# Relation attention of a graph kernel: four turns of two heads by 13 or 12 destination blocks in place of five turns of four heads by 5 blocks

## The chip, the cores and the metric

The kernel runs on one core of a Trainium2 chip. The metric is the device time of one execution in microseconds (us). Engines are named as in the profile: PE is TensorE (PEld its weight loads), DVE is VectorE, ACT is ScalarE, POOL is GpSimd, SP is SyncE, which here only issues DMAs.

## The reference

Four graph layers follow each other on 3125 nodes with 128 features and 103125 edges. The change touches the third one alone, an attention with three relations and four heads of 32 features:

```
for r in range(3):
    h = (x @ W[r]).reshape(N, 4, 32)
    a_s, a_d = einsum(h, att_src[r]), einsum(h, att_dst[r])      # [N, 4] each
    score = leaky_relu(a_s[src] + a_d[dst], 0.2); edges of another type masked, self edges kept
    alpha = softmax of score over the edges of a destination, per head
    rel_out = segment_sum(alpha * h[src], dst)
    out = out + softmax(rel_w)[r] * (rel_out + bias[r])
x = layernorm(x + out)
```

## The kernel before

Nodes are cut into 25 blocks of 125. Earlier in the kernel the edges are counted into matrices `K.counts[r]` in DRAM: for each source node (partition), destination block and source block, a row of 128 16-bit counts. Attention is then dense: since leaky_relu has two branches, the exponential of a score is a product of a source factor and a destination factor on either side of a threshold. For each pair of blocks and each head the kernel makes `sel`, the counts where the destination's `ad` is on one side of the source's threshold, and multiplies it on PE with the values `T.mv` (each split in two 16-bit parts); the other side comes as the unmasked counts `ct` times the values less the same.

For each of the three relations (tags `r0`, `r1`, `r2`) `gat` runs `scores` (projection, thresholds, values; it also loads the first `ct` and `ad` tiles), then `attention_heads`, then `relation_sum`, one after the other; each is a block that all engines leave together.

`attention_heads` has five turns, a loop over g. In a turn five destination blocks sit in PSUM banks 0 to 4 (264 columns each, for four heads), and 25 steps run over the source blocks s. In a step

- ACT makes the masks of three heads (two in steps 7, 15 and 23) by a Sigmoid with a very large scale (L936), 640 columns each;
- DVE makes the other one or two heads' `sel` with a compare and multiply of 640 columns (L954) and multiplies the ACT masks with the counts (L958, 1920 or 1280 columns);
- PE runs, for each of the 5 blocks, eight matmuls of 66 columns (four heads, two parts; L1009) and two of 132 columns with the unmasked counts (L1013).

`sel` and `msk` have five slots by step. DVE runs three steps into the next turn and then drains the five banks (L969 multiplies by the destination factors, L976 adds the two halves). PE clears a bank with a matmul of zeros (L1005) at a turn's first step, after that bank was drained. SP loads `ct` in chunks of five source blocks (L925) and the next turn's `ad` (L919).

`relation_sum` divides by the denominators and adds the result to `K.x` (L1061 to L1066); for r0 it also adds the bias (L1070 to L1074).

Of the kernel before, what the change touches and what calls it, by code (L numbers as in the profile page):

```python
# [217 lines left out]
def count_edges(nc, K, S):  # L218
# [12 lines left out]
    with ExitStack() as ctx:  # L231
# [9 lines left out]
        with nc.Block() as block:  # L241
# [48 lines left out]
            def _(pe):  # L290
# [31 lines left out]
                with pe.Else():  # L322
                    pe.sem_inc(wide_used, 1)

                    def five_groups(i):
                        for s in range(OHS):

                            pe.wait_ge(taken, i * OHS + s + 1)
                            pe.matmul(K.ps[:, s, :], K.zeros[:, 0:128], K.zeros[:], start=True, stop=True)
# [7 lines left out]
                            pe.matmul(K.ps[:, s, 0:128], K.zeros[:, 0:128], K.zeros[:, 0:128], start=False, stop=False,  # L337
# [278 lines left out]
def scores(nc, K, S, tag, k, counts, H, F, T):  # L616
# [9 lines left out]
    with ExitStack() as ctx:  # L626
# [17 lines left out]
        with nc.Block() as block:  # L644
# [45 lines left out]
            @block.sync  # L690
            def _(sp):

                for c in range(5):
                    sp.dma_start(T.ct[:, c], counts[:, 0:5, 5 * c:5 * c + 5]).then_inc(T.landed[c], 16)
                sp.wait_ge(adt, 7)
                sp.dma_start(K.ad_rows[0:H], adr[:]).then_inc(adst, 16)
                sp.wait_ge(adst, 16)
                sp.sem_inc(T.ad_landed, 16)
# [55 lines left out]
def attention_one(nc, K, S, tag, counts, F, T, degree=False):  # L754
# [6 lines left out]
    with ExitStack() as ctx:  # L761
# [31 lines left out]
        with nc.Block() as block:  # L793
# [69 lines left out]
            def _(pe):  # L863
                pe.sem_inc(used, 25)
                with pe.Fori(0, 5) as g:
                    for s in range(NB):
# [3 lines left out]
                        for b in range(5):  # L870
                            if s == 0:

                                pe.wait_ge(drained, 5 * g + b + 1)
                                pe.matmul(K.ps[:, b, 0:2 * F], K.zeros[:, 0:128], K.zeros[:, 0:2 * F], start=True,
                                          stop=True)
# [11 lines left out]
def attention_heads(nc, K, S, tag, counts, H, F, T):  # L887
# [7 lines left out]
    AHEAD = 3  # L895
    HF = H * F

    by_act = lambda s: list(range(2 if s % 8 == 7 else 1, H))
    masks = [sum(len(by_act(i)) for i in range(s)) for s in range(NB + 1)]
    with ExitStack() as ctx:  # L900
        sb = lambda name, shape, dt: ctx.enter_context(nc.sbuf_tensor(tag + name, shape, dt))
        ct, ad, landed, ad_landed = T.ct, T.ad, T.landed, T.ad_landed
        sel = sb("sel", [P, 5, H, 5, PAD], F16)
        msk = sb("msk", [P, 5, 3, 5, PAD], F16)
        tmp = sb("tmp", [P, 2, 2 * HF], F32)
        (masked, used, full, scaled, drained, mready, turns) = (
            S(tag + "_" + n) for n in ("masked", "used", "full", "scaled", "drained", "mready", "turns"))
        with nc.Block() as block:
            @block.sync
            def _(sp):  # L910

                with sp.Fori(1, 5) as g:

                    slot, first = sp.snap(g % 2), sp.snap(5 * g)
                    made, had = sp.snap(25 * g + 1), sp.snap(16 * g + 16)
                    ready_first(sp, slot, first, made, had)
                    sp.wait_ge(used, made)
                    sp.wait_ge(ad_landed, had)
                    sp.dma_start(ad[:, bass.ds(slot, 1)].rearrange("p a h d -> p (a h) d"),  # L919
                                 K.ad_rows[0:H, bass.ds(first, 5)].rearrange("h b d -> h (b d)").partition_broadcast(P)  # L920
                                 ).then_inc(ad_landed, 16)
                    for c in range(5):

                        sp.wait_ge(used, 25 * g + 5 * c + 5)
                        sp.dma_start(ct[:, c], counts[:, bass.ds(first, 5), 5 * c:5 * c + 5]).then_inc(landed[c], 16)  # L925

            @block.scalar
            def _(act):
                with act.Fori(0, 5) as g:
                    for s in range(NB):  # L930
                        act.wait_ge(ad_landed, 16 * g + 32)

                        act.wait_ge(masked, 25 * g + s + 1)
                        act.sem_inc(turns, 1)
                        for n, h in enumerate(by_act(s)):
                            act.activation(msk[:, s % 5, n], ad[:, bass.ds(g % 2, 1), h]  # L936
                                           .rearrange("p a (b d) -> p (a b) d", d=PAD),
                                           ACT.Sigmoid, bias=T.thr[:, 1, s, h:h + 1],
# [3 lines left out]
            def _(v):  # L942
                v.sem_inc(drained, 5)
                v.sem_inc(masked, 5)

                def step(g, s):

                    n, c = len(by_act(s)), ct[0:P, s // 5, :, s % 5]
                    v.wait_ge(ad_landed, 16 * g + 32)
                    v.wait_ge(landed[s // 5], 16 * g + 16)  # L950

                    v.wait_ge(used, 25 * g + s + 21)
                    for h in range(H - n):
                        v.scalar_tensor_tensor(  # L954
                            sel[:, s % 5, h], ad[:, bass.ds(g % 2, 1), h].rearrange("p a (b d) -> p (a b) d", d=PAD),
                            T.thr[:, 0, s, h:h + 1], c, ALU.is_lt, ALU.mult)
                    v.wait_ge(mready, masks[NB] * g + masks[s + 1])
                    v.tensor_tensor(sel[:, s % 5, H - n:H], msk[:, s % 5, 0:n],  # L958
                                    c.unsqueeze(1).to_broadcast([P, n, 5, PAD]), ALU.mult).then_inc(masked, 1)

                def drain(g):

                    for b in range(6):
                        if b < 4:
                            v.wait_ge(full, 4 * g + b + 1)
                        elif b == 4:
                            v.wait_ge(used, 25 * g + 50)
                        if b < 5:
                            v.tensor_tensor(tmp[:, b % 2].rearrange("p (x f) -> p x f", f=F),  # L969
                                            K.ps[0:P, b, 0:2 * HF].rearrange("p (x f) -> p x f", f=F),  # L970
                                            T.c[:, bass.ds(5 * g + b, 1)].rearrange("p b h a -> p (b h a)").unsqueeze(2)
                                            .to_broadcast([P, 2 * H, F]), ALU.mult).then_inc(drained, 1)
                        if b > 0:
                            v.wait_ge(drained, 5 * g + b + 5)
                            t4 = tmp[:, (b - 1) % 2].rearrange("p (h a f) -> p h a f", h=H, a=2)
                            v.tensor_tensor(T.num[:, bass.ds(5 * g + b - 1, 1)].rearrange("p b h f -> p (b h) f"),  # L976
                                            t4[:, :, 0], t4[:, :, 1], ALU.add).then_inc(scaled, 1)
                            v.wait_ge(scaled, 5 * g + b)

                for s in range(AHEAD):  # L980
                    step(0, s)
                with v.Fori(0, 4) as g:
                    for s in range(AHEAD, NB):
                        step(g, s)
                    for s in range(AHEAD):
                        step(g + 1, s)
                    drain(g)
                for s in range(AHEAD, NB):
                    step(4, s)
                drain(4)  # L990

            @block.tensor
            def _(pe):
                pe.sem_inc(used, 25)
# [663 lines left out]
```

## Time and profile before

| | |
|---|---|
| median of 3 runs | 2834.3 us (2833.37 to 2838.01) |
| the profiled execution: its time | 2861.55 us |
| its span, first to last instruction | 2859.7 us |
| PE busy | 73% of the span |
| DVE busy | 78% |
| ACT busy | 64% |
| mean granted clock of PE | 0.888 |

The profiled execution is 27 us longer than the median of the runs without a profiler. Sums below are made against its own time. "Busy" counts an instruction from its start to its end; instructions of one engine overlap by a little, so the pitch from start to start is what adds up.

### The profile page before, as it was taken

To read this page: it belongs to the slowest core of one execution; us is meant where nothing else is said; L and a number is where in the kernel's file an instruction comes from. 1 tells how busy PE (TensorE), PEld (TensorE's weight loads), DVE (VectorE), ACT (ScalarE), POOL (GpSimd) and SP (SyncE) were. 2 spreads that over 40 slices of the span, in tenths; PEclk is the share of its full clock that TensorE was granted. 3 is DMA by queue.
4 is the path that set the end of the run, shared out by engine and by line. 5 is a ranking of instruction groups with operands and counts; after the bars stand their busy time and mean duration, and the time that the engine had idled before them with its cause. 6 is when DMAs were issued, how large, how long until landed. Compare 5 with 4: busy or idle time off the path is not lost. (4 is left out here: it accounts for less than half of the span.)

```text
span 2859.7 us, 90081 instructions
## 1 busy us (share of the span) xinstructions
PE 2092.1 (73%) x33857; PEld 1846.2 (65%) x33857; DVE 2223.9 (78%) x4347; ACT 1831.8 (64%) x3004; POOL 158.2 (6%) x143
## 2 busy tenths in 40 slices
PE   0069978949959959939593998768995898766644
PEld 0045544638949949839482898768994898656622
DVE  2999978958878878761517999889997999849953
ACT  0059977957757666520205999599996999535421
POOL 0331133100000000000000000000000000000000
PEclk9979999979979979969796999889997999878867
DMA  2224534544314324227262333043312333034100
GB/s 80 87 86 189 229 158 163 225 159 125 123 63 142 106 90 147 73 65 226 77 210 77 107 102 91 17 127 95 108 56 81 104 101 97 8 105 128 57 8 23
DMA packets 186835, 308.74 MB, mean 108 GB/s; under 512 B 6718, under 2 KB 163265, under 8 KB 186446
## 3 DMA queue, kind: packets, MB, share of 16 engines
q1 hardware_dynamic: 185626, 303.77, 32.1%
q8 instruction: 204, 3.34, 0.5%
q0 software_dynamic: 960, 1.26, 0.2%
q14 instruction: 45, 0.37, 0.0%
HBM read 220.45 MB, written 88.67 MB: 108 GB/s over the span
## 5 line engine op out<-in xcount | busy, mean ns | idle before, releaser
L372 ACT ACTIVATE stage<-ps 125x375 f32 x625 | 314.0, 604 | 150.5 <-PE ps L317 146.1
L270 DVE TENSOR_SCALAR col<-iota_col,window_col 125x376 bf16<-125x376 f16 x1250 | 334.4, 336 | 33.4 <-PE ps L317 33.4
L317 PE MATMUL ps<-col,lo 125*125 125x375 bf16 x1250 | 288.1, 346 | 41.9 <-DVE col L270 41.7
L936 ACT ACTIVATE r2amsk<-r2ad,r2thr 125x640 f16 x360 | 259.9, 815 | 0.4 <-DVE r2asel L958 0.3
L936 ACT ACTIVATE r0amsk<-r0ad,r0thr 125x640 f16 x360 | 259.6, 814 | 0.1
L936 ACT ACTIVATE r1amsk<-r1ad,r1thr 125x640 f16 x360 | 259.6, 815 | 0.1
L1009 PE MATMUL ps<-r2mv,r2asel 125*128 125x66 f16 x5000 | 244.1, 196 | 6.6 <-issue 5.4
L317 PEld LDWEIGHTS ps<-col,lo 125*125 125x125 bf16 x1250 | 140.8, 141 | 163.0 <-DVE col L270 157.5
L1009 PE MATMUL ps<-r1mv,r1asel 125*128 125x66 f16 x5000 | 243.3, 196 | 2.7 <-issue 1.6
L1009 PE MATMUL ps<-r0mv,r0asel 125*128 125x66 f16 x5000 | 243.1, 196 | 1.3 <-DVE r0asel L958 0.5
L1009 PEld LDWEIGHTS ps<-r2mv,r2asel 125*128 125x128 f16 x5000 | 227.4, 100 | 10.4 <-issue 5.9
L1009 PEld LDWEIGHTS ps<-r1mv,r1asel 125*128 125x128 f16 x5000 | 226.8, 100 | 6.3 <-DVE r1asel L958 2.8
L1009 PEld LDWEIGHTS ps<-r0mv,r0asel 125*128 125x128 f16 x5000 | 226.6, 100 | 4.7 <-DVE r0asel L958 3.3
L1013 PE MATMUL ps<-r0mv,r0ct 125*128 125x132 f16 x1250 | 180.9, 228 | 5.1 <-issue 5.1
L1013 PE MATMUL ps<-r2mv,r2ct 125*128 125x132 f16 x1250 | 180.5, 228 | 0.0
L1013 PE MATMUL ps<-r1mv,r1ct 125*128 125x132 f16 x1250 | 180.1, 228 | 0.0
L1178 PE MATMUL ps<-parts,ct 125*128 125x128 f16 x2500 | 151.1, 222 | 35.8 <-DVEq L1187 33.0
L1178 PEld LDWEIGHTS ps<-parts,ct 125*128 125x128 f16 x2500 | 143.9, 100 | 43.1 <-DVEq L1187 33.5
L303 PE MATMUL ps<-stage,ident 125*125 x756 | 130.8, 309 | 37.6 <-ACT total L361 33.9
L878 PE MATMUL ps<-g0mv,g0asel 125*128 125x130 f16 x2500 | 147.8, 220 | 0.0
L878 PE MATMUL ps<-g2mv,g2asel 125*128 125x130 f16 x2500 | 147.3, 220 | 0.0
L878 PE MATMUL ps<-g1mv,g1asel 125*128 125x130 f16 x2500 | 147.1, 219 | 0.0
(532 smaller groups left out, 4480.8 us busy)
## 6 DMA issues: line engine op xcount, KB each, us to landing
counts<-stage SPq DMA_DIRECT2D x75, 800.0 KB, 4.8
ct<-counts_all SPq DMA_DIRECT2D x75, 800.0 KB, 4.6
counts_all<-total SPq DMA_DIRECT2D x25, 800.0 KB, 7.3
g0ct<-counts_all SPq DMA_DIRECT2D x25, 800.0 KB, 4.5
g1ct<-counts_all SPq DMA_DIRECT2D x25, 800.0 KB, 4.5
g2ct<-counts_all SPq DMA_DIRECT2D x25, 800.0 KB, 4.6
r0ct<-counts SPq DMA_DIRECT2D x25, 800.0 KB, 5.1
r1ct<-counts SPq DMA_DIRECT2D x25, 800.0 KB, 4.7
```

The source lines that it names most:

```text
L270: ins = v.tensor_scalar(col1[:, b % OHS * WIN + w], K.iota_col[:], K.window_col[:, bass.ds(i * (P // DG) + b, 1), w], None, ALU.is_equal)
L303: ins = pe.matmul(K.ps[0:P, OHS + half, 0:(h1 - h0) * NB], K.ident16[0:P, 0:P], stage[0:P, bass.ds(slot, 1), r, h0:h1, bass.ds(25 * q, 25) ...
L317: ins = pe.matmul(K.ps[0:P, s, 0:GW], lo1[:, b, 0:P, w], col1[:, s * WIN + w, 0:GW], start=(w == 0), stop=(w == WIN - 1))
L372: act.activation(dst.rearrange("p a r h d -> p (a r h) d"), K.ps[0:P, b % OHS, 0:GW].rearrange("p (x d) -> p x d", d=DG), ACT.Copy).then_i ...
L878: ins = pe.matmul(K.ps[:, b, a * F:(a + 1) * F], sel[:, s % 5, a, b], T.mv[:, s, (2 * p + a) * F:(2 * p + a + 1) * F], start=False, stop=F ...
L936: act.activation(msk[:, s % 5, n], ad[:, bass.ds(g % 2, 1), h] .rearrange("p a (b d) -> p (a b) d", d=PAD), ACT.Sigmoid, bias=T.thr[:, 1, ...
L1009: pe.matmul(K.ps[:, b, 2 * h * F:2 * (h + 1) * F], sel[:, s % 5, h, b], vs[:, (h * 2 + p) * 2 * F:(h * 2 + p + 1) * 2 * F], start=False, s ...
L1013: ins = pe.matmul(K.ps[:, b, 0:2 * HF].rearrange("p (h a f) -> p h a f", h=H, a=2)[:, :, 1], ct[0:P, s // 5, b, s % 5], vs[:, (4 + p) * HF ...
L1178: ins = pe.matmul(K.ps[:, b, 0:D], ct[0:P, s // 5, b, s % 5], parts[:, s, p], start=(s == 0 and p == 0), stop=(s == NB - 1 and p == 1))
```

## The change

- Turns: four in place of five, as a list. A turn takes two of the four heads and 13 or 12 destination blocks: heads 0 and 1 with blocks 0 to 12, the same heads with blocks 13 to 24, then heads 2 and 3 likewise. Three blocks share a PSUM bank (396 columns); turns use banks 1, 2, 3, 4, 0 and 5, 6, 7, 0 in alternation.
- The unit of work is one source block and one head, so 50 units in a turn, 200 in a relation. `sel` and `msk` have five slots by unit. Each mask has 13 or 12 times 128 columns. DVE makes the mask of every fifth unit itself, ACT the other 40 of a turn.
- PE's matmuls with unmasked counts have 66 columns in place of 132 and there are twice as many; those with `sel` stay at 5000.
- Drains of a turn are spread over the next turn's units 2 to 6, one bank behind each, and behind them `add_to_rows` divides and adds this turn's part to `K.x` at once. `relation_sum` is gone. r0's bias is added ahead of the first unit.
- `ct` holds three chunks of five source blocks in place of five, and every count is loaded twice in a relation. `ad` is loaded on 128 partitions in place of 125, for two heads and 13 blocks.
- All loops over turns are written out; `attention_one` and the other phases are as before, but that the zeros have 128 partitions, of which 125 are used.

```
+    PAIR = 2 * F
+    UNITS = 2 * NB
...
+    TURNS = [(hp, b0, nb, banks) for hp in range(2) for b0, nb, banks in ((0, 13, (1, 2, 3, 4, 0)), (13, 12, (5, 6, 7, 0)))]
+    released = [sum(len(t[3]) for t in TURNS[:k]) for k in range(len(TURNS) + 1)]
+    by_dve = lambda u: u % 5 == 0
+    masks = [k * (UNITS - UNITS // 5) for k in range(len(TURNS) + 1)]
+    before = [sum(not by_dve(i) for i in range(u)) for u in range(UNITS + 1)]
...
+                for k, (hp, b0, nb, banks) in enumerate(TURNS):
+                    if k > 0:
+                        if k > 1:
+                            sp.wait_ge(masked, UNITS * (k - 1))
+                        load_ad(sp, K, T, TURNS, k)
                     for c in range(5):
+                        q = 5 * k + c
+                        if q >= 3:
+                            sp.wait_ge(used, 10 * (q - 2))
+                            sp.dma_start(ct[:, q % 3, 0:nb], counts[:, b0:b0 + nb, 5 * c:5 * c + 5]).then_inc(landed[q % 3], 16)
...
+                for k, (hp, b0, nb, banks) in enumerate(TURNS):
+                    act.wait_ge(ad_landed, 16 * k + 16)
+                    for u in range(UNITS):
+                        if not by_dve(u):
+                            m = masks[k] + before[u]
+                            if m >= 5:
+                                old = m - 5
+                                j = old // masks[1]
+                                act.wait_ge(masked, UNITS * j + before.index(old - masks[j] + 1))
+                            act.activation(msk[:, m % 5, 0:nb], ad[0:P, k % 2, u % 2, 0:nb], ACT.Sigmoid,
+                                           bias=T.thr[:, 1, u // 2, 2 * hp + u % 2:2 * hp + u % 2 + 1],
                                            scale=-STEEP).then_inc(mready, 1)
...
+                def step(k, u):
+                    hp, b0, nb, banks = TURNS[k]
+                    n, s, h, q = UNITS * k + u, u // 2, u % 2, 5 * k + u // 10
+                    if u % 10 == 0:
+                        v.wait_ge(landed[q % 3], 16 * (q // 3) + 16)
+                    if n >= 5:
+                        v.wait_ge(used, n - 4)
+                    c = ct[0:P, q % 3, 0:nb, s % 5]
+                    if by_dve(u):
+                        if u == 0:
+                            v.wait_ge(ad_landed, 16 * k + 16)
+                        v.scalar_tensor_tensor(sel[:, n % 5, 0:nb], ad[0:P, k % 2, h, 0:nb],
+                                               T.thr[:, 0, s, 2 * hp + h:2 * hp + h + 1], c, ALU.is_lt,
+                                               ALU.mult).then_inc(masked, 1)
+                    else:
+                        m = masks[k] + before[u]
+                        v.wait_ge(mready, m + 1)
+                        v.tensor_tensor(sel[:, n % 5, 0:nb], msk[:, m % 5, 0:nb], c, ALU.mult).then_inc(masked, 1)
+                def drain(k, i):
+                    hp, b0, nb, banks = TURNS[k]
+                    order = sorted(range(len(banks)), key=lambda i: banks[i])
+                    i, first = order[i], i == 0
+                    n, x = min(3, nb - 3 * i), released[k] + order.index(i)
+                    if first:
+                        v.wait_ge(used, UNITS * (k + 1))
+                    v.tensor_tensor(tmp[:, x % 2, 0:n].rearrange("p b h a f -> p b (h a) f"),
+                                    K.ps[0:P, banks[i], 0:n * 2 * PAIR].rearrange("p (b x f) -> p b x f", b=n, f=F),
+                                    T.c[:, b0 + 3 * i:b0 + 3 * i + n, 2 * hp:2 * hp + 2].rearrange("p b h a -> p b (h a)")
+                                    .unsqueeze(3).to_broadcast([P, n, 4, F]), ALU.mult).then_inc(drained, 1)
+                    v.wait_ge(drained, x + 1)
+                    v.tensor_tensor(num[:, 3 * i:3 * i + n], tmp[:, x % 2, 0:n, :, 0], tmp[:, x % 2, 0:n, :, 1],
+                                    ALU.add).then_inc(summed, 1)
+                def add_to_rows(k):
+                    hp, b0, nb, banks = TURNS[k]
+                    v.wait_ge(summed, released[k + 1])
+                    link(v.reciprocal(rden[:, 0:nb], num[:, 0:nb, :, F - 1]))
+                    link(v.tensor_scalar(rden[:, 0:nb], rden[:, 0:nb], wr, T.top[:], ALU.mult, ALU.mult))
+                    link(v.tensor_tensor(num[:, 0:nb, :, 0:F - 1], num[:, 0:nb, :, 0:F - 1],
+                                         rden[:, 0:nb].unsqueeze(3).to_broadcast([P, nb, 2, F - 1]), ALU.mult))
+                    own_x = K.x[:, b0:b0 + nb, 64 * hp:64 * hp + 64].rearrange("p b (h f) -> p b h f", h=2)
+                    link(v.tensor_tensor(own_x, own_x, num[:, 0:nb, :, 0:F - 1], ALU.add))
...
+                for k in range(len(TURNS)):
+                    for u in range(UNITS):
+                        step(k, u)
+                        if k > 0 and 0 <= u - LEAD < len(TURNS[k - 1][3]):
+                            drain(k - 1, u - LEAD)
+                        if k > 0 and u - LEAD == len(TURNS[k - 1][3]):
+                            add_to_rows(k - 1)
+                for i in range(len(TURNS[-1][3])):
+                    drain(len(TURNS) - 1, i)
+                add_to_rows(len(TURNS) - 1)
...
+                for k, (hp, b0, nb, banks) in enumerate(TURNS):
+                    place = lambda i: (banks[i // 3], i % 3 * 2 * PAIR)
+                    for u in range(UNITS):
+                        n, s, h, q = UNITS * k + u, u // 2, u % 2, 5 * k + u // 10
+                        pe.wait_ge(masked, n + 1)
                         vs = T.mv[:, s]
+                        for i in range(nb):
+                            bank, at = place(i)
+                            if u == 0 and i % 3 == 0:
+                                if bank == 0 and k > 0:
+                                    pe.wait_ge(drained, released[k - 1] + 1)
+                                elif k > 1:
+                                    pe.wait_ge(drained, released[k - 1])
+                                w = min(3, nb - i) * 2 * PAIR
+                                pe.matmul(K.ps[:, bank, 0:w], K.zeros[0:P, 0:128], K.zeros[0:P, 0:w], start=True, stop=True)
+                            for p in range(2):
+                                x = (2 * (2 * hp + h) + p) * PAIR
+                                ins = pe.matmul(K.ps[:, bank, at + h * PAIR:at + (h + 1) * PAIR], sel[:, n % 5, i],
+                                                vs[:, x:x + PAIR], start=False, stop=False, skip_group_check=True)
+                        if h == 1:
+                            if s % 5 == 0:
+                                pe.wait_ge(landed[q % 3], 16 * (q // 3) + 16)
+                            for i in range(nb):
+                                bank, at = place(i)
                                 for p in range(2):
+                                    x = (4 + p) * HF + hp * PAIR
+                                    ins = pe.matmul(K.ps[:, bank, at:at + 2 * PAIR]
+                                                    .rearrange("p (h a f) -> p h a f", h=2, a=2)[:, :, 1],
+                                                    ct[0:P, q % 3, i, s % 5],
+                                                    vs[:, x:x + PAIR].rearrange("p (h f) -> p h f", h=2),
+                                                    start=False, stop=False, skip_group_check=True)
                         ins.then_inc(used, 1)
...
+def load_ad(sp, K, T, turns, k):
+    hp, b0, nb, banks = turns[k]
+    sp.dma_start(T.ad[:, k % 2, :, 0:nb], K.ad_rows[2 * hp:2 * hp + 2, b0:b0 + nb].partition_broadcast(ROWS)
+                 ).then_inc(T.ad_landed, 16)
```

## Rows read from the trace of the kernel before

**Rows 1.** Busy time of each engine over stretches: the relations' attention, then their sums.
```profile
core 0: us, PE busy (x) PEld busy (x) DVE busy (x) ACT busy (x) POOL busy (x), PEclk, DMA share, GB/s
1562.40:1842.50 280.10, 250.59 (x6275) 245.65 (x6275) 258.02 (x315) 266.05 (x365) 0.00 (x0) 0.94 0.27 80
1842.50:1855.80 13.30, 0.00 (x0) 0.00 (x0) 12.57 (x8) 0.00 (x0) 0.00 (x0) 0.53 0.00 0
1886.50:2162.50 276.00, 250.45 (x6275) 245.59 (x6275) 257.85 (x315) 266.05 (x365) 0.00 (x0) 0.95 0.28 81
2162.50:2171.30 8.80, 0.00 (x0) 0.00 (x0) 8.11 (x5) 0.00 (x0) 0.00 (x0) 0.59 0.00 0
2203.20:2484.00 280.80, 251.38 (x6275) 246.65 (x6275) 258.16 (x315) 266.29 (x365) 0.00 (x0) 0.94 0.28 80
```

**Rows 2.** ACT's groups by line: shapes, count, busy us, mean ns, idle before.
```profile
L936 ACT ACTIVATE r0amsk<-r0ad,r0thr 125x640 f16 x360 | 259.6, 814 | 0.1
...
L680 ACT ACTIVATE r0mv<-r0sval 125x1320 f16<-125x1320 f32 x10 | 13.0, 1303 | 1.3 <-DVE r0sval L738 0.5
...
L1149 ACT ACTIVATE parts<-ks 125x640 f16<-125x640 f32 x5 | 3.2, 724 | 0.0
```

**Rows 3.** DVE in order of time, in turn 0: start, us, instruction.
```profile
1612.14 1.16 DVE L958 TENSOR_TENSOR r0asel<-r0amsk,r0ct 125x1920 f16<-125x1920 f16 x1 [0.21 <-ACT r0amsk L936]
1613.21 1.68 DVE L954 SCALAR_TENSOR_TENSOR r0asel<-r0ad,r0thr,r0ct 125x640 f16<-125x640 f16 x2
1614.81 0.82 DVE L958 TENSOR_TENSOR r0asel<-r0amsk,r0ct 125x1280 f16<-125x1280 f16 x1
```

**Rows 4.** PE in order of time, the first work of turn 1.
```profile
1625.19 0.40 PE L1005 MATMUL ps<-zeros 125*128 125x264 bf16 x1 [5.57 <-DVE r0atmp L969]
```

**Rows 5.** PE in order of time, second and fourth blocks of turn 0, PE slow and then fast.
```profile
1569.33 0.65 PE L1009 MATMUL ps<-r0mv,r0asel 125*128 125x66 f16 x8
1569.79 0.42 PE L1013 MATMUL ps<-r0mv,r0ct 125*128 125x132 f16 x2
...
1570.66 0.42 PE L1009 MATMUL ps<-r0mv,r0asel 125*128 125x66 f16 x8
1570.92 0.28 PE L1013 MATMUL ps<-r0mv,r0ct 125*128 125x132 f16 x2
```

**Rows 6.** DVE in order of time, from the last drains into the sum.
```profile
1841.26 0.43 DVE L969 TENSOR_TENSOR r0atmp<-ps,r0c 125x264 f32<-125x264 f32 x1
1841.61 0.61 DVE L976 TENSOR_TENSOR r0num<-r0atmp 125x132 f32<-125x132 f32 x2
1842.77 0.78 DVE L1061 RECIPROCAL r0nrden<-r0num 125x100 f32<-125x100 f32 x1 [0.54 <-PEq L908]
1843.58 0.33 DVE L1062 TENSOR_SCALAR r0nrden<-r0nrden,relw,r0top 125x100 f32<-125x100 f32 x1
1843.95 3.49 DVE L1063 TENSOR_TENSOR r0num<-r0num,r0nrden 125x3200 f32<-125x3200 f32 x1
```

**Rows 7.** Waits of the engines in r0's attention: us in total, times, longest.
```profile
PE ps L1013 <- issue: 5.1, 3, 2.0
```

**Rows 8.** Waits of the engines in r2's attention.
```profile
PE ps L1009 <- issue: 5.4, 5, 1.6
```

**Rows 9.** DMA queues from 1525 to 1855 us: packets, MB, share of 16 engines.
```profile
q8 instruction: 59, 0.97, 1.3%
```

**Rows 10.** DMA from 1536 to 1546 us, while `ct` is loaded.
```profile
DMA packets 2915, 3.66 MB, mean 366 GB/s; under 512 B 64, under 2 KB 2914, under 8 KB 2914
```

**Rows 11.** DMA from 1549.5 to 1562 us, while `ad` is loaded.
```profile
DMA packets 505, 1.28 MB, mean 102 GB/s; under 512 B 5, under 2 KB 5, under 8 KB 505
```

More of the change, by code:

```diff
@@ L902, in attention_heads @@
         ct, ad, landed, ad_landed = T.ct, T.ad, T.landed, T.ad_landed
[L903 to L907, printed above, removed]
+        sel = sb("sel", [P, 5, 13, PAD], F16)
+        msk = sb("msk", [P, 5, 13, PAD], F16)
+        tmp = sb("tmp", [P, 2, 3, 2, 2, F], F32)
+        num = sb("num", [P, 13, 2, F], F32)
+        rden = sb("rden", [P, 13, 2], F32)
+        (masked, used, drained, summed, own, mready) = (
+            S(tag + "_" + n) for n in ("masked", "used", "drained", "summed", "own", "mready"))
         with nc.Block() as block:
@@ L942, in _ @@
             def _(v):
[L943 to L990, printed above, removed]
+                link = Chain(v, own)
+                wr = K.relw[0:P, 3 + r:4 + r]
+                def step(k, u):
[16 more added lines that the diff above has]
+                        v.tensor_tensor(sel[:, n % 5, 0:nb], msk[:, m % 5, 0:nb], c, ALU.mult).then_inc(masked, 1)
@@ new lines, in _ @@
+                if r == 0:
+                    bias = K.rows[0:P, 0:D]
+                    link(v.tensor_scalar(bias, bias, wr, None, ALU.mult))
+                    for i in range(1, R):
+                        link(v.scalar_tensor_tensor(bias, K.rows[0:P, i * D:(i + 1) * D], K.relw[0:P, 3 + i:4 + i], bias,
+                                                    ALU.mult, ALU.add))
+                    link(v.tensor_tensor(K.x[:], K.x[:], bias.unsqueeze(1).to_broadcast([P, NB, D]), ALU.add))
+                for k in range(len(TURNS)):
[5 more added lines that the diff above has]
+                            add_to_rows(k - 1)
@@ L1485, in build, with relation @@
                 count_edges(nc, K)
+        def relation(tag, r):
+            with ExitStack() as c3:
+                sb3 = lambda name, shape, dt: c3.enter_context(nc.sbuf_tensor(tag + name, shape, dt))
+                T.mv = sb3("mv", [P, NB, 6 * 4 * 33], F16)
+                T.top = sb3("top", [P, 1], F32)
+                T.thr = sb3("thr", [P, 2, NB, 4], F32)
+                T.c = sb3("c", [P, NB, 4, 2], F32)
+                T.ct = sb3("ct", [ROWS, 3, 13, 5, PAD], F16)
+                T.ad = sb3("ad", [ROWS, 2, 2, 13, PAD], F32)
+                T.landed = [nc.alloc_semaphore(f"{tag}_landed{c}") for c in range(3)]
+                T.ad_landed = nc.alloc_semaphore(tag + "_ad_landed")
+                scores(nc, K, tag + "s", 3 + r, K.counts[r], 4, 33, T)
+                attention_heads(nc, K, tag + "a", K.counts[r], 4, 33, T, r)
         def gat(tag, k, H, F, counts, finish, degree=False):
```

94 lines of the change are left out of this document (13 added, 81 removed).

## The prediction

> **What bounds the kernel now.** I read the busy times by stretch first. The three relations' attention takes 280.1, 276.0 and 280.8 us and the sum behind each another 13.3, 8.8 and about 8.7 us (r2 repeats r1): 868 us, nearly a third of the kernel [rows 1]. The reader is to see that ACT is busy 266 us of each 276 to 281, against 258 of DVE and 251 of PE, and that in the sums only DVE works. The groups of ACT confirm it: 360 masks fill 259.6 us, 0.721 us from start to start for a duration of 0.814, with 0.1 us of idle time in all [rows 2]. The rest of ACT's 266 us is a table load for each loop turn. So ACT sets the pace of a step, 3 x 0.721 = 2.16 us. DVE's order of time shows the same from the other side: each L958 first waits 0.2 us for ACT [rows 3]. PE comes last in the chain and stands still 5.6 us at the turn, for DVE runs three steps ahead and drains only then [rows 4]. What follows ACT's last mask is a tail: PE's last steps, five drains, the division.
>
> **The new work, engine by engine, for one relation.**
>
> ACT: 160 masks, 80 of 1664 and 80 of 1536 columns. The trace has no such length. Two activations without pointer operands give the slope, (1303 - 724)/(1320 - 640) = 0.85 ns a column [rows 2]. From 0.721 us at 640 columns a mask then costs 1.59 or 1.48 us: 246 us, and one table load 1.3 us, 247.5 us. That is 18.5 less than before; what is saved is the fixed part of 200 instructions and four table loads, less 11% more columns.
>
> DVE: the 16-bit product costs (1.16 - 0.82)/640 = 0.53 ns a column and starts 1.07 us after the last at 1920 columns [rows 3], so 0.93 or 0.87 us for a unit. The compare is 0.80 us from start to start at 640 columns (two of them take 1.68 us); at the 32-bit slope of (3.49 - 0.30)/(3200 - 132) = 1.04 ns [rows 3, 6] it is 1.87 or 1.73 us. A turn has 40 and 10 of them: 55.9 or 52.1 us, 216 us in all. A drain multiplies 396 columns (0.43 + 0.14) and adds 198 (0.29 + 0.07); with 0.08 us overlap and 0.03 of hand-over I take 0.88 us, sixteen full and two small ones (0.47) being 15 us. A division is 0.3 + 0.3 us of small work and two passes over 832 or 768 columns at 1.0 us: 2.7 us, 10.8 in all [rows 6]. DVE has 242 us. The division's work is not less than in the old sum; three quarters of it now lie beside ACT and PE.
>
> PE: eight matmuls of 66 columns start within 0.26 us, 32.5 ns each, when PE is fast [rows 5]. After the change all 7500 have 66 columns: 243.8 us, and 18 clearings of up to 396 columns at no more than 0.2 us, 3 us. PE has 247 us. It was not at its bound before; now its sum equals ACT's, and DVE's is only 2% below. Per five units ACT needs 6.4 us (5.9 at 12 blocks), PE 6.3 (5.9), DVE 5.6 (5.2) without its drains.
>
> **What the queues add.** (a) Start: DVE's first compare, 2.0 us, then PE begins, against 5 us before, when PE waited for three ACT masks; the next units wait for ACT's first masks and PE begins slow, 2.5 us more. In r0 the bias work (0.3 + 2 x 0.4 + 3.5 us) now stands ahead of the first compare; ACT's first masks cover little of it: 4 us more. (b) The turns. The first drain waits until PE has ended the old turn, and DVE has then made units 0 to 2 of the new one, worth 3.8 us of PE with the clearings. Behind it DVE owes a drain and a unit alternately and then the division: units 3, 4, 5, 6, 7, 8 are ready at 1.4, 3.1, 5.7, 7.5, 9.2 and 12.7 us, where PE would like them at 3.8, 5.4, 6.2, 7.7, 8.5 and 10.8 at the latest. So unit 5 to 7 come at about PE's pace, with 0.7 us lost, unit 8 is 1.9 us late, and bank 0, which both turns use, costs some 0.5. I take 3.4 us for each of three turns, 10 us; ACT meanwhile fills its five mask slots, five times 1.5 us, and does not stop. Before, a turn cost PE 5.6 us, but there ACT's pace counted, so that it showed only in the tail. (c) End: four drains and a division, 6.3 us, against 3.4 for the drains, 0.5 to leave the block and 8.1 for the sum. Together 2.0 + 247 + 2.5 + 10 + 6.3 = 268 us for r1 and r2 and 272 for r0: 808 us against 868, 60 us less.
>
> **DMA.** Counts are now loaded twice, 41 MB a relation, with rows of the same 1280 bytes. At 366 GB/s [rows 10] that is 112 us of 268, 5.8 us a chunk of 2.13 MB, while a chunk's slot comes free two chunks (25 us) ahead: hidden. At the start three chunks, 6.4 MB, take 17.5 us from 1535.6 on, and the write of `ad` to DRAM queues behind them. The new `ad` load, 1.7 MB, then starts near 1557.5 us. Its rate is the unknown: as the old one on 125 partitions, about 1.28 MB in 11 us [rows 11], it takes 14 us and holds ACT for 9 us of r0 and some 5 of the others; at that of the counts, which also go to 128 partitions, it takes 4.7 us and lands as the phase begins. I take the latter, and keep 19 us for the range. The Trainium skill ("DMA: Bandwidth & Descriptors", "Why a DMA increments its semaphore by 16 and not by 1") says that a transfer uses the largest number of engines up to 16 that divides its slowest dimension, hence 5 for 125 partitions and 16 for 128; the trace's two rates agree with it.
>
> **Instruction supply.** PE waited for nothing the profile shows three times in r0 (5.1 us) and five times in r2 (5.4 us) [rows 7, 8], while 59 packets of instructions came, 0.97 MB in r0's stretch [rows 9]. Before, most of this was hidden behind ACT's pace; now it is PE's time. The code is straight, but has 15,000 PE instructions against 12,500, and the DMA queues carry twice the counts. Between nothing and 6 us a relation I take 2: 6 us in all.
>
> **The forecast.** 2861.55 - 60 + 6 = 2807.6 us for a profiled execution; against the median of the runs, 2834.3 - 54 = 2780 us, 1.9% less.
>
> **Rivals.**
> - ACT stays the bound. PE's sum passes ACT's by nothing I can measure, and the pitch of 32.5 ns is read in blocks that mix 66 and 132 columns; if in a stream of 66 alone it is 31 or less, PE needs under 236 us, catches up after each turn, and ACT's 247.5 with start (2), one late unit a turn (1) and the tail (8) sets 260 us a relation, 26 us less in all, 2754. Chance 0.13. The Trainium skill ("TensorE: Matmul & The Clock Gate", "Back-to-back issue gap") gives columns/2.4 + 2.5 ns for a fast PE, 30.0 ns for 66 columns, by which PE would have 228 us and this rival would hold; [rows 5] show 32.5.
> - The turns cost more. Three engines with equal sums and five short slots (6.3 us of PE, where five steps were 10.8) leave nothing to catch up with: if the drains and the division (6.5 us of DVE) stop PE in full, 3 x 3 us more a relation, and ACT's slots fill too, 2 us a turn: 27 to 45 us less gain, 2807 to 2825. Speaks for it: PE's idle time at each old turn [rows 4]. Against: units 0 to 2 are made before. Chance 0.2.
> - No change: the two losses above, `ad` and the turns, together with PE's instruction waits as large as in r0. Chance 0.05.
> - Slower: the instruction supply. By the count of instructions some 71 packets a relation replace 59, one each 3.8 us instead of 4.7, while chunks of 2.13 MB fill the queues for 5.8 us. With 213 packets in all a mean lateness of 0.3 us each eats the 60 us, and from 0.32 on the kernel is slower; at 0.5 us it is 2880. The old trace has eight such waits in two relations, 0.09 us a packet. The Trainium skill ("Runtime: NRT & Kernel Launch", "Instruction fetch mechanics") says that blocks are fetched ahead in a straight line and that a taken branch stalls; by it the waits vanish and the sum is 6 us lower. Chance 0.07.
>
> The forecast itself holds 0.55, its own range 2765 to 2797. A measurement tells 0.2%, 6 us, from no change. Faster by more than that: 0.55 + 0.13 + 0.2 = 0.88; the same 0.05; slower 0.07. The range runs from 2750 (ACT the bound) to 2815, which takes in the slower `ad` load and most of the costlier turns.
>
> **What would show it.** ACT's groups: masks of 1664 columns at a mean of 1.69 us (pitch 1.59); DVE's products at 1.02 us and compares at 1.95; PE's matmuls 32.5 ns apart, those of the counts too; PE idle 2 to 4 us at each turn and little elsewhere; ACT no longer without idle time, since five slots hold it to DVE; 268 us from a phase's first compare to its last addition. Wrong would be: PE slow (at the half clock) inside turns, since there each matmul starts after 57 ns (eight in 0.46 us) [rows 5]; long "issue" waits on PE; ACT's first mask of a relation late behind `ad`.

## The result: 0.6% slower

The changed kernel takes 2852.68 us (median, 2849.73 to 2855.06) against 2834.22 us beside it on the same chip: a ratio of 1.0064, interval 1.005 to 1.0079. Forecast were 2780 us and 2750 to 2815. The changed kernel's profiled execution has 2855.06 us (span 2853.3), close to its median; that of before was 27 us above its own because its counting phase, outside the change, was longer. So spans are compared here by relation, not over the kernel. From r0's first compare to its last addition r0 takes 293.2 us, r1 295.2 and r2 295.0 where 268 were forecast; in the kernel before the same stretches take 288.6, 284.7 and 289.5.

Busy time by stretch, from PE's first matmul of a relation to about its last, the columns as in [rows 1]:

```profile
1541.20:1827.00 285.80, 251.96 (x7518) 246.91 (x7518) 239.00 (x241) 241.58 (x157) 0.00 (x0) 0.96 0.43 141
1866.00:2154.00 288.00, 251.55 (x7518) 246.53 (x7518) 239.67 (x241) 246.35 (x160) 0.00 (x0) 0.96 0.42 140
```

ACT's busy time fell as meant, from 266 us to about 247, and DVE's from 258 to 240. Yet the stretch is 286 to 288 us, longer than before: no engine is busy even nine tenths of it. There is no bound by work now; the time is in waits. The waits of r0's attention (total, times, longest), which answer to [rows 7]:

```profile
ACT r0amsk L944 <- DVE r0asel L971: 34.7, 29, 2.9
...
PE ps L1035 <- DVE r0asel L965: 23.2, 1, 23.2
...
PE ps L1038 <- issue: 17.1, 11, 2.6
DVE r0asel L965 <- PE ps L1047: 14.4, 11, 3.2
...
DVE r0asel L971 <- PE ps L1047: 11.6, 18, 1.7
PE ps L1047 <- issue: 11.3, 8, 2.1
DVE r0atmp L981 <- PE ps L1047: 9.3, 4, 4.9
DVE r0asel L965 <- issue: 5.3, 3, 2.7
```

The 23.2 us are the time before PE's first work. The two "issue" rows of PE are the finding: 19 times, 28.4 us in all, PE stood still though it waited for no other engine, where [rows 7] have three times and 5.1 us. r1 has 30.1 and r2 29.5 us of it; r2's part, answering to [rows 8]:

```profile
PE ps L1038 <- issue: 24.6, 14, 2.9
```

The rest of the list follows from it for the most part. When PE stops, the five slots fill, so DVE waits for PE (14.4 and 11.6 us), then ACT for DVE (34.7 us; 10.0 are left in e3 below, where the instructions come in time). DVE itself has "issue" waits of up to 2.7 us (5.3, 6.4 and 3.3 us in the three relations, none in the kernel before); how much of the time is due to them no run tells apart. PE in order of time at one such place (start, us, instruction, idle time before it), its fast pitch answering to [rows 5]:

```profile
1561.21 1.78 PE L1038 MATMUL ps<-r0mv,r0asel 125*128 125x66 f16 x52
1562.83 0.98 PE L1047 MATMUL ps<-r0mv,r0ct 125*128 125x66 f16 x26
1563.65 1.25 PE L1038 MATMUL ps<-r0mv,r0asel 125*128 125x66 f16 x35
1566.37 0.70 PE L1038 MATMUL ps<-r0mv,r0asel 125*128 125x66 f16 x17 [1.47 <-issue]
```

A unit of 52 matmuls is cut in the middle, after its 35th. Nothing in the program waits there; the reading, which the experiments below bear out, is that the next instruction was not there yet. The DMA view tells what was going on: SP issued a count load at 1556.53. First the stretch from 1557.1 to 1563.9, ahead of the gap, then as long a one from 1563.9 to 1570.7:

```profile
DMA packets 1629, 2.08 MB, mean 306 GB/s; under 512 B 2, under 2 KB 1629, under 8 KB 1629
...
q1 hardware_dynamic: 1629, 2.08, 94.6%
```
```profile
q1 hardware_dynamic: 51, 0.05, 2.2%
q8 instruction: 2, 0.03, 2.0%
```

While the 2.13 MB chunk fills the queues no instruction packet starts; in the next stretch of the same length two do. The single records say when: packets of 16 KB start at 1557.01 and then at 1564.00, 7.0 us apart, where a PE that hardly waits takes one each 4.0 us (the median in r0 of e3, below). At the next three loads the packets' starts look alike (1570.87 to 1577.52, 1585.17 to 1591.13, 1598.27 to 1604.67), and behind each of the four PE stands still for 1.5 us. There are 17 such loads in a relation; r0's 28.4 us are 1.7 us for each, the single waits up to 2.6. The number of packets did not grow, though 71 were forecast for a relation (r0 with its start, by queue; compare [rows 9]):

```profile
q1 hardware_dynamic: 28320, 40.81, 40.2%
q8 instruction: 59, 0.97, 1.4%
```

### The profile page after: what moved, and what is told of

Its sections match the earlier page's. It is cut to its first block and busy times, and to the rows that moved or that the text cites. A ratio compares the mean times of both kernels' runs of the same rounds, so it can differ in the third digit from the quotient of the medians.

```text
span 2853.3 us, 94270 instructions
## 1 busy us (share of the span) xinstructions
PE 2094.4 (73%) x37586; PEld 1843.9 (65%) x37586; DVE 2167.0 (76%) x4146; ACT 1778.9 (62%) x2392; POOL 121.1 (4%) x143
## 5 line engine op out<-in xcount | busy, mean ns | idle before, releaser
L944 ACT ACTIVATE r0amsk<-r0ad,r0thr 125x1664 f16<-125x1664 f32 (+1 forms) x160 | 246.9, 1618 | 34.9 <-DVE r0asel L971 34.7
L944 ACT ACTIVATE r2amsk<-r2ad,r2thr 125x1664 f16<-125x1664 f32 (+1 forms) x160 | 247.6, 1617 | 31.9 <-DVE r2asel L971 31.5
L944 ACT ACTIVATE r1amsk<-r1ad,r1thr 125x1664 f16<-125x1664 f32 (+1 forms) x160 | 246.7, 1617 | 33.2 <-DVE r1asel L971 33.0
L1038 PE MATMUL ps<-r2mv,r2asel 125*128 125x66 f16 x5000 | 183.5, 195 | 29.8 <-issue 24.6
L1038 PE MATMUL ps<-r1mv,r1asel 125*128 125x66 f16 x5000 | 183.0, 195 | 23.3 <-issue 18.0
L1038 PE MATMUL ps<-r0mv,r0asel 125*128 125x66 f16 x5000 | 182.9, 195 | 21.6 <-issue 17.1
L971 DVE TENSOR_TENSOR r1asel<-r1amsk,r1ct 125x1664 f16<-125x1664 f16 (+1 forms) x160 | 152.5, 987 | 22.8 <-PE ps L1047 11.1
L971 DVE TENSOR_TENSOR r2asel<-r2amsk,r2ct 125x1664 f16<-125x1664 f16 (+1 forms) x160 | 152.4, 987 | 22.8 <-PE ps L1047 14.8
L971 DVE TENSOR_TENSOR r0asel<-r0amsk,r0ct 125x1664 f16<-125x1664 f16 (+1 forms) x160 | 151.8, 987 | 16.9 <-PE ps L1047 11.6
L881 PEld LDWEIGHTS ps<-g0mv,g0asel 125*128 125x128 f16 x2500 | 145.4, 97 | 0.6
```

Of the source, the lines that this page charges most:

```text
L881: ins = pe.matmul(K.ps[:, b, a * F:(a + 1) * F], sel[:, s % 5, a, b], T.mv[:, s, (2 * p + a) * F:(2 * p + a + 1) * F], start=False, stop=F ...
L944: act.activation(msk[:, m % 5, 0:nb], ad[0:P, k % 2, u % 2, 0:nb], ACT.Sigmoid, bias=T.thr[:, 1, u // 2, 2 * hp + u % 2:2 * hp + u % 2 + 1 ...
L971: v.tensor_tensor(sel[:, n % 5, 0:nb], msk[:, m % 5, 0:nb], c, ALU.mult).then_inc(masked, 1)
L1038: ins = pe.matmul(K.ps[:, bank, at + h * PAIR:at + (h + 1) * PAIR], sel[:, n % 5, i], vs[:, x:x + PAIR], start=False, stop=False, skip_gro ...
```

## The experiments

All were timed against the kernel before, on the same chip as the others of their group: e1 to e4, e5 to e8, e9 to e11. Across groups the ratios are what compares.

**e1 and e2: the same bytes, spread or together.** In both each count load is cut into five pieces by destination blocks. e1 issues each piece one step of two units behind the last; e2 issues all five at once, where the whole load was issued.

```
+    PIECES = ((0, 3), (3, 6), (6, 9), (9, 11), (11, 13))
...
+                            for j, (i0, i1) in enumerate(PIECES):
+                                sp.wait_ge(used, 10 * (q - 2) + 2 * j)      # e2: without "+ 2 * j"
+                                i1 = min(i1, nb)
+                                sp.dma_start(ct[:, q % 3, i0:i1], counts[:, b0 + i0:b0 + i1, 5 * c:5 * c + 5]).then_inc(
+                                    landed[q % 3], 16)
```

> Theory (late instructions): in the changed kernel PE waits for nothing the profile shows 28 to 30 us a relation, 1.7 us behind each of the 17 loads of 2.13 MB, whose packets fill the DMA queues for 7 us and hold back the next packet of instructions. Here each load is cut by destination blocks into five pieces of at most 0.49 MB, issued two units (2.5 us) apart; bytes and rows are the same. Expected: the instruction packets come every 4 us again, the waits without a releaser fall below 6 us a relation, and the kernel falls from 2853 to 2765 to 2785 us. Rival (the written-out PE code, 15,000 instructions a relation, is what is late): the waits stay at 28 us and the time at 2850.

> The same five pieces as in the run before, but all issued at once where the whole load stood, so that the queues are full as long as before. Theory (length of the burst): waits of 28 us a relation stay, 2845 to 2860 us. Rival (a large DMA instruction is what hurts, by its descriptors): the waits vanish and the time falls to 2775.

e1: 2801.77 us, 0.9901 (0.9885 to 0.9918) of before, PE's instruction waits 9.7, 10.5 and 10.8 us. e2: 2843.45 us, 1.0052 (1.0035 to 1.0069), waits 29.1, 24.6 and 25.0 us. So e1's waits and time stayed above what was expected of it (under 6 us and 2765 to 2785), and e2 lies just under its 2845 to 2860 with most of the waits kept. From the waits of r0, e1 (its `sel` matmuls alone; 9.7 with the others) and then e2:

```profile
PE ps L1043 <- issue: 6.4, 7, 2.3
```
```profile
PE ps L1043 <- issue: 17.4, 12, 2.4
...
PE ps L1052 <- issue: 11.7, 7, 2.6
```

Same pieces, same bytes, same number of DMAs: the 42 us between the two lie in the moments of issue alone. So it is the burst that costs most, not the size of one DMA, and 1.5% of time turns on it. That e1 still waits 10 us, with the traffic of the changed kernel, is more than e3 has without it.

**e3: no count loads.** Behind the first three chunks no count is loaded; the work is done on what stands in the slots, so that the output isn't the reference's.

```
                         if q >= 3:
                             sp.wait_ge(used, 10 * (q - 2))
-                            sp.dma_start(ct[:, q % 3, 0:nb], counts[...]).then_inc(landed[q % 3], 16)
```

> Leaves out every load of counts after the first three chunks of a relation; the later units use the three chunks that are there, so the output is not the reference's, while each engine does the same work. Theory (late instructions through the count loads): waits without a releaser below 5 us a relation, but for those behind the loads of ad; 2760 to 2780 us. Rival (the length of the code alone): still 28 us of such waits, 2850 us. If this is clearly faster than the spread loads, even short bursts cost something.

2768.32 us, 0.978 (0.9764 to 0.9797); the relations take 263.3, 268.7 and 264.3 us. The queues of r0 and PE's group:

```profile
q1 hardware_dynamic: 816, 4.85, 5.1%
q8 instruction: 59, 0.97, 1.4%
```
```profile
L1037 PE MATMUL ps<-r0mv,r0asel 125*128 125x66 f16 x5000 | 178.4, 194 | 8.6 <-DVE r0asel L970 8.3 <-DVE r0asel L964 0.2
L1046 PE MATMUL ps<-r0mv,r0ct 125*128 125x66 f16 x2500 | 96.7, 197 | 1.4 <-issue 1.4
```

The same 59 instruction packets now cost 1.4 us. With the loads gone the relations come out near the 268 us of the forecast, in part because errors of its terms offset each other (see the table below).

**e4: bursts in the kernel before.** Each count load of 0.82 MB is followed by two more of the same size into a tile that nobody reads.

```
+                        for w in range(2):
+                            sp.dma_start(spare[:, w], counts[:, bass.ds(first, 5), 5 * c:5 * c + 5]).then_inc(spared, 16)
```

> The kernel before, with each of its 60 loads of counts followed by two more of the same 0.82 MB into a spare tile that nobody reads: bursts of 2.4 MB, with the old turns and loops. Theory: PE's waits without a releaser rise from some 5 us to 25 to 40 us a relation (1.7 us for each of 20 bursts); part of it lies in the slack of 0.28 us that PE has in each step, so the time rises by 0 to 50 us over 2834, 2860 likeliest. Rival (the new code's length or its form is to blame): the waits stay at 5 us a relation and the time at 2834.

2893.1 us, 1.0238 (1.0209 to 1.0268). PE's instruction waits rose from 5.1, 1.6 and 8.9 us to 35.4, 18.3 and 32.4. The time rose by 62 us, more than the 0 to 50 expected. With 2.46 MB at a time the old order of work suffers in the same way; nothing in the new order is needed for it. (This run has three times the bytes as well as longer bursts; the two are told apart only by e1 and e2.)

**e5: finer still.** The counts of one destination block in a DMA (0.16 MB), spread evenly over the ten units of a chunk; the next turn's `ad` in five pieces between them.

```
+                        for i in range(nb):
+                            sp.wait_ge(used, 10 * (q - 2) + 10 * i // nb)
+                            sp.dma_start(ct[:, q % 3, i], counts[:, b0 + i, 5 * c:5 * c + 5]).then_inc(landed[q % 3], 16)
+                            if c == 4 and k < 3 and i % 2 == 0 and i < 10:
+                                load_ad(sp, K, T, TURNS, k + 1, i // 2)      # three blocks of ad
```

> Counts loaded one destination block at a time (0.16 MB, 13 or 12 pieces over the ten units of a chunk) and ad three blocks at a time between them, so that no burst is longer than about 1 us. Spread in five pieces the kernel took 2802 us and PE still waited 10 us a relation without a releaser, against 2 to 3 with no count loads (2768). Theory (what counts is how long the queues are full at a time): waits below 5 us a relation, 2768 to 2785 us. Rival (what counts is the number of bytes loaded beside the instructions): waits stay at 10 us, 2800 us.

2787.78 us, 0.9833 (0.9817 to 0.985): 65 us less than the changed kernel. Waits for instructions are 7.1, 6.7 and 6.8 us. Both lie a little above what was expected (below 5 us, 2768 to 2785). The queue of the data is busy for longer than in the changed kernel (40.2% there), and PE waits a quarter as long for instructions:

```profile
q1 hardware_dynamic: 33920, 39.43, 49.7%
q8 instruction: 59, 0.97, 1.4%
```

**e6: e5, and the division later.** `add_to_rows` is called behind unit 22 of the next turn in place of unit 6 or 7.

```
-                        if k > 0 and u - LEAD == len(TURNS[k - 1][3]):
+                        if k > 0 and u == 22:
                             add_to_rows(k - 1)
```

> The run before, with the division and addition of a turn behind unit 22 of the next instead of unit 7 or 6. Theory of the forecast (behind the drains the division makes unit 8 late by 1.9 us and costs 2 of 3.4 us a turn): 9 turns, PE's waits for DVE fall by 4 to 6 us a relation, 10 to 18 us faster than the run before. Rival (PE is behind DVE by then and does not notice): no change.

2760.04 us, 0.9738 (0.9721 to 0.9754), 27.7 us less than e5, more than was expected. The turn in the changed kernel, DVE and then PE (compare [rows 4]):

```profile
1621.09 0.31 DVE L992 RECIPROCAL r0arden<-r0anum 125x26 f32<-125x26 f32 x1
1621.44 0.30 DVE L993 TENSOR_SCALAR r0arden<-r0arden,relw,r0top 125x26 f32<-125x26 f32 x1
1621.77 1.03 DVE L994 TENSOR_TENSOR r0anum<-r0anum,r0arden 125x832 f32<-125x832 f32 x1
1622.83 1.03 DVE L997 TENSOR_TENSOR x<-x,r0anum 125x832 f32<-125x832 f32 x1
1623.89 1.83 DVE L971 TENSOR_TENSOR r0asel<-r0amsk,r0ct 125x1536 f16<-125x1536 f16 x2
```
```profile
1621.23 0.92 PE L1038 MATMUL ps<-r0mv,r0asel 125*128 125x66 f16 x24 [0.83 <-DVE r0asel L971]
1621.99 0.92 PE L1047 MATMUL ps<-r0mv,r0ct 125*128 125x66 f16 x24
1624.91 1.78 PE L1038 MATMUL ps<-r0mv,r0asel 125*128 125x66 f16 x48 [1.99 <-DVE r0asel L971]
```

The division stops PE for 1.99 us on top of the drains' 0.83. In e6 the drains' wait is left (0.82 us), and the division has a smaller one where it now stands, at unit 22:

```profile
1635.81 0.92 PE L1039 MATMUL ps<-r0mv,r0asel 125*128 125x66 f16 x24 [1.11 <-DVE r0asel L972]
```

In e5 the time behind PE's wait was lost too, in PE's clock. e5 at its first turn, PE in order of time:

```profile
1614.08 1.78 PE L1039 MATMUL ps<-r0mv,r0asel 125*128 125x66 f16 x48
...
1622.12 2.78 PE L1039 MATMUL ps<-r0mv,r0asel 125*128 125x66 f16 x48 [2.00 <-DVE r0asel L972]
```

The same 48 matmuls take 2.78 us behind the wait in place of 1.78: the granted clock was 0.84 from 1618 to 1629 us and 0.50, which is 1.2 GHz, from 1622.2 to 1625.6 of them. r0 as a whole, PE busy and granted clock of e5 and then e6:

```profile
1542.30:1804.00 261.70, 245.97 (x7517) 241.93 (x7518) 237.04 (x239) 239.80 (x157) 0.00 (x0) 0.98 0.53 155
```
```profile
1540.00:1793.60 253.60, 242.79 (x7516) 238.79 (x7517) 235.85 (x239) 239.31 (x157) 0.00 (x0) 0.99 0.55 160
```

3.2 us less of PE busy with the same matmuls, 3.0 less of waits for DVE and 1.9 less of waits for instructions: the 8.1 us by which r0 is shorter. Over the three relations PE busy gave 10 us, the waits for DVE 11 and those for instructions 7. The waits for DVE fell by 3 to 4 us a relation, less than the 4 to 6 expected; it is through the other two that the gain is larger than expected.

**e7 and e8: eight slots in place of five** for `sel` and `msk`, upon e5 and upon e6.

```
-                            if m >= 5:
-                                old = m - 5
+                            if m >= 8:
+                                old = m - 8
...
-                    if n >= 5:
-                        v.wait_ge(used, n - 4)
+                    if n >= 8:
+                        v.wait_ge(used, n - 7)
```

> The finer loads with eight slots of sel and msk in place of five, division where it was. Theory (a turn's delay is not caught up because five slots hold 6.3 us): DVE's waits for PE (23 us a relation with spread loads) fall to under 10, ACT's for DVE likewise, and PE's late units at the turns shrink little, since the first drain still waits for PE's last unit: 3 to 12 us faster than the finer loads. If the slots are what couples the engines, 20 us or more.

> Finer loads, eight slots and the late division together. If the three terms are separate the gains add: 2740 to 2765 us. If PE is the bound already without them, as its sum of 237 us (31.2 ns a matmul) and ACT's of 248 say, it stops near ACT's bound: 258 us a relation and about 2750.

e7: 2783.32 us, 0.9824 (0.9803 to 0.9845); e8: 2760.59 us, 0.9736 (0.9719 to 0.9752). Neither is told apart from its partner with five slots. DVE's and ACT's waits for a free slot looked large, but taking them away gained nothing that these runs can tell: they were the shadow of a PE that stood still.

**e9 and e10: the late division alone, and without the loads.** e9 is the changed kernel with the one edit of e6; e10 is e3 with it (output not the reference's).

> The changed kernel with one edit: the division of a turn's result is issued behind unit 22 of the next turn in place of unit 6 or 7, so that it no longer follows the drains directly. Count loads are whole, as in the changed kernel. With small loads the same edit gave 27.7 us. If that gain comes from the crowd at the turn alone, independent of the instruction supply, it is the same here: about 2825 us, ratio 0.996 to the kernel before. If slack on DVE merely let late instructions be caught up (the two losses share one slack), the gain is smaller, 5 to 15 us: 2838 to 2848. If the division now falls on a late-instruction gap and stops PE with it, nothing is gained: 2850 or more.

> The changed kernel without count loads after the first three chunks (the work is done on stale counts, so that the output isn't the reference's) and with the late division of unit 22. Leaving out the loads alone gave 2768 us, the small loads with the late division 2760 us. If the late division is worth 9 us a relation wherever the instructions come in time, this gives 2768 - 27 = 2741 us, and the small loads leave 19 us of supply losses still to be had. If the small loads have already taken all that there is, both sit on the sum of PE's or ACT's work and this gives 2755 to 2760.

e9: 2833.5 us, 0.9987 (0.9959 to 1.0014), 0.8% or some 22 us better than the changed kernel by the ratios, which lies between the 27 and the 5 to 15 us of its two expectations. e10: 2746.25 us, 0.9696 (0.9651 to 0.9741), again some 22 us below e3 and between the 2741 and the 2755 of its expectations. So the late division gains some 22 to 28 us with the bursts, with small loads and with none, by intervals that do not tell 22 from 28: it is a loss of its own. e6 lies some 12 us above e10 by the medians' ratios, whose intervals overlap a little; the profiled relations agree (262 us, e10's 256 to 259). That is about what the loads still cost. PE of r0 in e10:

```profile
L1037 PE MATMUL ps<-r0mv,r0asel 125*128 125x66 f16 x5000 | 177.1, 193 | 5.5 <-DVE r0asel L970 4.6 <-DVE r0asel L964 0.7
```

**e11: small loads in the kernel before.** Each 0.82 MB load is cut into five of one destination block, one step apart.

> The kernel before with one edit: each count load of 0.82 MB is cut into five loads of one destination block, each issued one step behind the last. PE's waits for instructions were 5.1, 1.6 and 8.9 us in the three relations, and ACT sets the pace, whose idle time is nearly nothing. If ACT's pace is what counts before, at most the part of the waits that ACT didn't cover is gained: 0 to 8 us, 2827 to 2835 (ratio 0.997 to 1.0). If the old kernel too is held by its instruction supply, its loss is up to 15 us: 2820, ratio 0.995.

2827.69 us, 0.9966 (0.9946 to 0.9986). The waits go from 5.1, 1.6 and 8.9 us to 4.5, 0 and 0.5. The old kernel lost little: its loads were short, and ACT's pace covered most. This is also the fair comparison for e5 and e6: with both orders of work fed in small pieces, the new one is 1.3% faster without the late division (0.9833 against 0.9966) and 2.3% with it (0.9738).

## Why the prediction was wrong

r0, term by term (us); a row's terms add up to its total within 0.7 us:

| | to PE's start | PE busy | waits for instructions | waits for DVE | behind PE | total |
|---|---|---|---|---|---|---|
| forecast | 2.0 | 247 + 2.5 slow start | 2 | 10 | 6.3 | 270 |
| changed kernel | 2.0 | 252.0 | 28.4 | 4.4 | 6.3 | 293.2 |
| e3, no loads | 2.0 | 244.8 | 1.4 | 8.5 | 6.3 | 263.3 |
| e5, small loads | 2.0 | 246.0 | 7.1 | 8.3 | 6.3 | 270.2 |
| e6, and late division | 2.0 | 242.8 | 5.2 | 5.3 | 6.3 | 262.1 |

**The step that failed** is "Instruction supply": 2 us a relation, "between nothing and 6". It measured 28.4, 30.1 and 29.5 us, 82 us more than forecast over the three; PE busy added 7 and smaller waits for DVE took 15 back. That makes 74 us, against 72 between forecast (54 less) and result (18 more). The text had the two facts, PE's waits of before and chunks of 2.13 MB that fill the queues for 5.8 us, and joined them in the rival it gave 0.07. That rival happened: 88 us of waits over 177 packets are 0.50 us each, above its point of 0.32. Its 2880 us at 0.50 were too many because it counted 213 packets. It had also read the old waits short: beside the 5.4 us of [rows 8] r2 has one more,

```profile
PE ps L1005 <- issue: 3.5, 1, 3.5
```

so that the kernel before waited 15.6 us in its three relations, and 2 us a relation for the new one was less than the old one's mean. What was missing above all was the link. The old waits were priced per packet, as an average; they should have been priced per load: how long does one load keep the queues full, how long does PE live on what it holds, and how often. A packet started just ahead of the burst and the next came 6 to 7 us later, where the pace of PE's work asks for one in 4.0.

**"Hidden"** was said of the count loads, and for the data it is true: no engine waited for `ct`. A DMA can be hidden for its own data and still be on the path through what it delays.

**ACT, DVE, the tail: right.** 80 masks of 1664 columns took a mean of 1.671 us and 80 of 1536 took 1.564 (forecast 1.69 for the first), 246.9 us in all (246); the rows that answer to [rows 2] and [rows 3]:

```profile
L944 ACT ACTIVATE r0amsk<-r0ad,r0thr 125x1664 f16<-125x1664 f32 x80 | 127.4, 1671 | 14.0 <-DVE r0asel L971 13.8
...
L971 DVE TENSOR_TENSOR r0asel<-r0amsk,r0ct 125x1664 f16<-125x1664 f16 x80 | 78.6, 1020 | 9.3 <-PE ps L1047 7.9 <-PE ps L1038 0.4
...
L965 DVE SCALAR_TENSOR_TENSOR r0asel<-r0ad,r0thr,r0ct 125x1664 f16<-125x1664 f32 x20 | 39.0, 1948 | 12.2 <-PE ps L1047 9.5 <-issue 2.7
```

DVE's product took 1.02 us (1.02) and its compare 1.95 (1.95), as [rows 3] gave. The tail, from the first of the last drains at 1826.13 to the last addition's end at 1832.39, is 6.3 us (6.3).

**PE's pitch: too high.** 78 matmuls from 1561.21 to 1563.65 are 31.3 ns each, not 32.5: 7500 need 235 us, 9 less. (The 30.0 ns that the prediction gives from the Trainium skill, "TensorE: Matmul & The Clock Gate", "Back-to-back issue gap", are nearer. The section gives that formula for a matmul by itself and says that it comes out too low at few columns when a weight load goes with each; here it is low by 1.3 ns.) The changed kernel gave this back at the half clock: its busy time is 252.0 us at a granted clock of 0.96, e10's 242.0 at 0.99. One of its longest gaps shows how (PE in order of time, then the next gap but for one line):

```profile
1643.68 0.92 PE L1047 MATMUL ps<-r0mv,r0ct 125*128 125x66 f16 x24
...
1647.70 1.33 PE L1038 MATMUL ps<-r0mv,r0asel 125*128 125x66 f16 x31 [2.57 <-issue]
1648.84 1.55 PE L1047 MATMUL ps<-r0mv,r0ct 125*128 125x66 f16 x24
```

The same 24 matmuls take 1.55 us behind the gap, 0.92 ahead of it; the granted clock was 0.50 from 1648.5 to 1651.9. r0 has five such stretches. The prediction named the half clock inside turns and long "issue" waits as signs that it was wrong; both were there.

**The rival that ACT stays the bound** needed a pitch of 31 or less and gave 260 us a relation. In the changed kernel it did not come about: the pitch is 31.3 ns, and no engine was the bound. With the supply and the late division mended, e6 (262) and e10 (256 to 259) end there; in r0 of e10 ACT's masks are busy for 244.2 us with 3.2 us of idle time, PE for 242.0.

**The turns:** 10 us were forecast; e3 has 8.5 us of PE's waits for DVE in r0. The forecast's late unit 8 (1.9 us) is the wait of 1.99. But it was wrong that ACT "does not stop": at the first turn of the changed kernel it waited 2.78 and 2.10 us for a slot. And the forecast costed the division beside the drains and did not ask whether it had to be there at all; it had 40 units of time.

**`ad`** was no loss: ACT's first mask of r0 started at 1535.86 without a wait, ahead of DVE's first compare at 1539.22.

Why a burst holds the instruction packets back (the same DMA engines, the memory, the order in a queue) no run here tells. Nor was it tried how large a piece may be: 0.33 to 0.49 MB spread left 10 us a relation, 0.16 MB 7, and no loads at all (e3) 1.4 to 3.5.

## What to carry to other kernels

Where an engine works off long straight code, look in the trace at its "issue" waits and at when the loads were issued: cut large loads into pieces, and above all issue the pieces apart. It gained 65 us of 2853 here without one byte less. When three engines have nearly equal sums, there is no slack to take up a wait, and a wait of PE can cost again in its clock behind it; work that nobody waits for, like a division of finished rows, belongs away from the turn. And a forecast that says "hidden" of a transfer owes a sentence on what shares the queues with it.

## What the runs showed of the hardware

- A load of 2.13 MB at 306 GB/s and more kept PE's next 16 KB of instructions away for 6 to 7 us, and PE lost 1.5 us at each of r0's first four loads and 1.7 on average. The Trainium skill ("Runtime: NRT & Kernel Launch", "Instruction fetch mechanics") has the instruction stream refilled on its own and the cost of a block boundary mostly hidden. The trace agrees where the queues are quiet (1.4 us in 59 packets in e3) and not beside bursts (28.4 us in as many).
- In r0 of the changed kernel PE's clock fell five times to 1.2 GHz (granted clock 0.50) for more than 3 us: within 1.2 us of the end of waits for instructions of 2.57, 2.01, 2.11 and 1.98 us, and at the end of two shorter waits in quick order (1.29 and 1.34 us). Behind the wait of 1.99 us for DVE that ended at 1624.91 the clock stayed at 2.4 GHz, as it did behind waits of 2.02, 2.03 and 2.06 us for instructions in r0 of e2. So the length of a wait alone does not tell here.
